# A gated cross-attention and ternary feed-forward block: the context projections of all four batches ahead of the first gate product, with every engine's order written anew

## The reference

```python
qp = ctx @ Wq.T + bq;  kp = ctx @ Wk.T + bk
scores = qp @ kp.T * 128**-0.5 * layernorm(x)
scores = where(mask, -inf, scores)
x = x + tanh(g0) * softmax(scores)
# feed-forward, weights ternary, activations scaled to 127 and rounded, row by row
gate = silu(qlinear(layernorm(x), w_gate))     # 512 -> 2048
up   = qlinear(layernorm(x), w_up)             # 512 -> 2048
x = x + tanh(g1) * qlinear(gate * up, w_down)  # 2048 -> 512
# qlinear: wq = clip(round(w / (mean|w| + eps)), -1, 1); xq = round(x / (max|x| / 127 + eps))
```

## Time and profile before

| | |
|---|---|
| time of the profiled execution | 218.4 us |
| its span | 216.6 us |
| TensorE busy | 201.9 us, 93% |
| VectorE busy | 185.9 us, 86% |
| ScalarE, POOL busy | 116.0 us, 102.0 us |
| mean granted TensorE clock | 0.976 of full speed |
| DMA | 32.84 MB, mean 152 GB/s |

### The profile page before, as it was taken

The page is one execution under the profiler, slowest core; times in us unless marked ns, Lnnn a source line. Parts: engine busy times, 40 slices in busy tenths (PEclk is TensorE's granted clock), DMA queues, the critical chain, the costliest instruction groups (busy, mean ns, idle before and its releaser), DMA issues.

```text
span 216.6 us, 2892 instructions
## 1 busy us (share of the span) xinstructions
PE 201.9 (93%) x862; PEld 91.4 (42%) x862; DVE 185.9 (86%) x376; ACT 116.0 (54%) x161; POOL 102.0 (47%) x152
## 2 busy tenths in 40 slices
PE   8866289999999999999999999999999999999983
PEld 7322133444444444444444444444444444444431
DVE  0899999899999999999999999999999859865711
ACT  2149988999889572296034572765442611532400
POOL 2657898880989696249732053175220520500000
PEclk9999758999999999999999999999999999999999
DMA  6999993089201380992031458002615251739991
GB/s 207 413 425 410 417 390 136 0 331 407 91 0 38 77 157 0 185 229 48 0 73 26 82 114 194 0 0 50 123 22 102 42 105 33 175 65 320 246 272 58
DMA packets 47360, 32.84 MB, mean 152 GB/s; under 512 B 40944, under 2 KB 41072, under 8 KB 45808
## 3 DMA queue, kind: packets, MB, share of 16 engines
q1 hardware_dynamic: 47200, 32.51, 52.6%
q10 hardware_dynamic: 144, 0.13, 0.4%
HBM read 18.48 MB, written 4.19 MB: 105 GB/s over the span
## 4 chain that ended last, share of the span: by engine, by line
PE 76%; DMA 11%; SPq 7%; DVE 2%; ACT 1%; ACTq 1%; issue 1%
PE pU L1024 25%; PE pG L1009 24%; PE pD L1043 21%; DMA stage_b<-in_L_ffn_w_up 9%; PE pA L976 4%; SPq L387 3%; DMA stage_b<-stage_b 2%; SPq L382 2%; ACTq L70 1%; PE pA L966 1%; PE pA L956 1%; SPq L374 1%; ACT hid L781 1%; DVE am L1385 1%; DVE hid L1381 1%
## 5 line engine op out<-in xcount | busy, mean ns | idle before, releaser
L781 ACT ACTIVATE hid<-pG,act_g 128x512 f32<-128x512 f32 x64 | 42.9, 686 | 50.2 <-PE pG L1009 41.3
L1009 PE MATMUL pG<-gate_w,xqT 128*128 128x512 f16 x256 | 62.6, 383 | 0.1
L1043 PE MATMUL pD<-down_w,stage_b 128*128 128x512 f16 x256 | 60.2, 379 | 1.1 <-DMA stage_b<-stage_b 1.1
L1024 PE MATMUL pU<-up_w,xqT 128*128 128x512 f16 x256 | 60.8, 379 | 0.0
L1376 DVE TENSOR_TENSOR hid<-pU,hid 128x512 f32<-128x512 f32 x64 | 42.1, 682 | 3.3 <-PE pU L1024 3.1
L1009 PEld LDWEIGHTS pG<-gate_w,xqT 128*128 128x128 f16 x256 | 25.0, 99 | 35.1 <-issue 7.4
L1043 PEld LDWEIGHTS pD<-down_w,stage_b 128*128 128x128 f16 x256 | 24.8, 98 | 32.5 <-issue 2.3
L1024 PEld LDWEIGHTS pU<-up_w,xqT 128*128 128x128 f16 x256 | 24.8, 98 | 30.7 <-issue 1.1
L976 PE MATMUL pA<-kT,qT 128*128 128x512 f32 x26 | 15.5, 679 | 4.5 <-DVE probs L1293 4.3
L1385 DVE TENSOR_REDUCE am<-hid 128x1 f32<-128x1025 f32 x16 | 19.3, 1211 | 0.3
L1381 DVE TENSOR_REDUCE hid<-hid 128x1 f32<-128x1024 f32 x16 | 19.3, 1206 | 0.0
(11 more groups left out here) (108 smaller groups left out, 245.7 us busy)
## 6 DMA issues: line engine op xcount, KB each, us to landing
stage_a<-in_L_ffn_w_gate SPq DMA_DIRECT2D x4, 1024.0 KB, 11.2
stage_b<-in_L_ffn_w_up SPq DMA_DIRECT2D x4, 1024.0 KB, 20.2
stage_a<-in_L_ffn_w_down SPq DMA_DIRECT2D x4, 1024.0 KB, 9.9
stage_b<-in_x SPq DMA_DIRECT2D x2, 1024.0 KB, 5.9
out<-x SPq DMA_DIRECT2D x8, 256.0 KB, 2.6
out<-stage_b SPq DMA_DIRECT2D x8, 256.0 KB, 3.4
ctx_s<-in_ctx SPq DMA_DIRECT2D x4, 256.0 KB, 8.6
x<-in_x SPq DMA_DIRECT2D x2, 512.0 KB, 5.6
```

The costliest lines, as they stand in the source:

```text
L781: act.activation(hid[:, t % NH, n * 512:(n + 1) * 512], pG[c % NG][:, :], ACT.Silu, scale=act_g[:, t:t + 1]).then_inc(silu_done, 1)
L1009: ins = pe.matmul(pG[c % NG][:, :], xqT[:, t // TILES % 2, t % TILES, k, :], gate_w[:, n, k, :], start=k == 0, stop=k == KD - 1)
L1024: ins = pe.matmul(pU[c % NU][:, :], xqT[:, t // TILES % 2, t % TILES, k, :], up_w[:, n, k, :], start=k == 0, stop=k == KD - 1)
L1043: ins = pe.matmul(pD[t % ND][:, :], hidT[:, t % 2, k, :], down_w[:, k // KD, k % KD, :], start=k == 0, stop=k == KI - 1)
```

## The change

The four products and copies for batches 2 and 3 leave pA. All q projections after the first go through bank pG1, all k projections through pG0, one after the other, and `gate(0, 0)` and `gate(1, 0)`, which are the first gate products to write these banks, wait for the copies of the last batch. `PA_ORDER` then holds only q0 and the scores.

```diff
-        q_banks = [pA, pG[1], pA, pA]
-        k_banks = [pG[0], pG[0], pA, pA]
+        q_banks = [pA, pG[1], pG[1], pG[1]]
+        k_banks = [pG[0], pG[0], pG[0], pG[0]]
...
-        CENTRE_BY = 'VPAAVAPAAPVAAVPA'
+        CENTRE_BY = 'VPAAPAPAAPVAAPPA'
...
-        HQ_BY = ['PA', 'AP', 'VP', 'PA', 'PV', 'VA', 'AP', 'VA', 'PA', 'VA', 'VP', 'PV', 'PP', 'AA', 'VV', 'AA']
+        HQ_BY = ['PA', 'AP', 'VP', 'PA', 'PV', 'AA', 'AP', 'VA', 'AA', 'VA', 'AP', 'PV', 'PP', 'VA', 'PV', 'AA']
...
-        SIGN_BY = ['VQQQ', 'QXQX', 'QXVQ']
+        SIGN_BY = ['VQQQ', 'QXQX', 'XXVQ']
...
             def project_q(b):
                 if b == 0:
                     pe.wait_ge(params_loaded, 16)
-                if b != 1:
-                    wait_pA(pe, "q", b)
+                    wait_pA(pe, "q", 0)
+                if b >= 2:
+                    pe.wait_ge(q_ready[b - 1], 1)
...
             def project_k(b):
...
-                if b >= 2:
-                    wait_pA(pe, "k", b)
-                elif b == 1:
-                    pe.wait_ge(k_ready[0], 1)
+                if b >= 1:
+                    pe.wait_ge(k_ready[b - 1], 1)
...
                 if c == 0:
-                    pe.wait_ge(k_ready[1], 1)
+                    pe.wait_ge(k_ready[B - 1], 1)
                 elif c == 1:
-                    pe.wait_ge(q_ready[1], 1)
+                    pe.wait_ge(q_ready[B - 1], 1)
```

More of the change, by code:

```diff
@@ L648, in _ @@
             residual1(6)
+            centre(4)
+            up_scales(1)
             std2(2)
@@ L653, in _ @@
             mask(2)
[L654 removed]
+            quantise_hidden(0, 0)
             gate_scales(2)
[L656 removed]
+            up_scales(2)
+            mask(3)
+            centre(6)
             std2(3)
[L658 to L659 removed]
+            weight_round(2, 3)
             quantise_hidden(1, 1)
@@ L857, in _ @@
             exp(11)
+            silu(6, 0)
+            silu(6, 1)
             silu(6, 2)
+            quantise_hidden(3, 1)
+            centre(8)
             silu(6, 3)
-            quantise_hidden(3, 1)
+            quantise_x(8)
             silu(7, 0)
             silu(7, 1)
-            centre(8)
-            quantise_x(8)
             silu(7, 2)
@@ L1180, in _ @@
             down(5, 2)
-            down(5, 3)
+            gate(9, 3)
+            up(8, 2)
+            up(8, 3)
+            up(9, 0)
             score(15)
@@ L1496, in _ @@
+            score(5)
+            weight_bound(0, 0)
             weight_bound(0, 1)
+            weight_bound(0, 2)
             absmax_x(2)
+            absmax_x(3)
             weight_abs(1, 3)
-            weight_bound(0, 2)
+            inverse_x(1)
+            stats1(6)
             weight_bound(0, 3)
-            absmax_x(3)
-            inverse_x(1)
             weight_scale(1)
-            inverse_std2(1)
-            stats1(6)
+            mask_and_max(5)
             score(6)
             stats1(7)
+            copy_xT(1)
@@ L1508, in _ @@
+            mask_and_max(6)
             weight_bound(1, 0)
             weight_bound(1, 1)
-            copy_xT(1)
             score(7)
+            mask_and_max(7)
             product(0, 0)
-            mask_and_max(4)
-            mask_and_max(5)
-            mask_and_max(6)
-            mask_and_max(7)
             product(1, 0)
             product(0, 1)
+            product(1, 1)
+            inverse_std2(1)
             weight_bound(1, 2)
-            product(1, 1)
             weight_bound(1, 3)
-            absmax_hidden(0, 0)
+            stats1(8)
@@ L1569, in _ @@
             score(10)
+            absmax_hidden(2, 0)
             weight_bound(2, 1)
-            inverse_hidden(2)
+            weight_round(2, 2)
+            score(11)
             weight_bound(2, 2)
             weight_bound(2, 3)
-            quantise_hidden(2, 0)
-            product(4, 2)
             product(4, 3)
-            absmax_hidden(3, 0)
-            residual2(0)
-            score(11)
-            mask_and_max(8)
-            mask_and_max(9)
+            absmax_hidden(2, 1)
@@ L1605, in _ @@
             absmax_x(8)
             absmax_x(9)
+            inverse_hidden(4)
             inverse_x(4)
+            quantise_hidden(4, 1)
+            stats2(10)
+            stats1(12)
+            inverse_std2(4)
+            score(12)
+            absmax_hidden(5, 0)
+            centre(10)
+            product(6, 3)
             product(7, 0)
-            quantise_hidden(4, 1)
+            mask_and_max(12)
             product(7, 1)
-            stats2(11)
-            product(7, 2)
-            absmax_hidden(5, 1)
@@ L1614, in _ @@
-            residual2(2)
-            inverse_hidden(5)
-            inverse_std2(4)
-            inverse_std2(5)
-            product(7, 3)
-            stats1(12)
-            centre(10)
-            absmax_x(10)
-            product(8, 0)
+            product(7, 2)
+            residual2(2)
+            stats1(13)
+            absmax_hidden(5, 1)
+            product(7, 3)
+            inverse_hidden(5)
+            absmax_hidden(6, 0)
+            stats2(11)
+            product(8, 0)
+            absmax_hidden(6, 1)
@@ L1636, in _ @@
-            inverse_hidden(6)
-            score(13)
-            inverse_hidden(7)
-            quantise_hidden(7, 0)
-            residual2(4)
-            stats1(14)
-            score(14)
-            mask_and_max(12)
-            stats1(15)
+            inverse_x(5)
+            absmax_hidden(8, 0)
+            stats1(14)
+            quantise_x(10)
+            residual2(4)
+            inverse_hidden(6)
+            stats1(15)
+            score(14)
+            product(8, 2)
+            absmax_hidden(7, 1)
@@ L1685, in _ @@
+            reciprocal_scale(6)
+            absmax_x(15)
+            absmax_hidden(11, 0)
+            inverse_x(7)
             product(11, 3)
             product(12, 0)
+            quantise_x(13)
+            inverse_std2(7)
+            absmax_hidden(11, 1)
+            product(12, 1)
+            inverse_hidden(9)
+            inverse_hidden(10)
+            product(12, 2)
+            product(12, 3)
+            inverse_hidden(11)
             quantise_hidden(9, 0)
-            absmax_hidden(10, 0)
```

603 lines of the change are left out of this document (286 added, 317 removed).

## The result

The changed kernel takes 220.71 us, the median of 4 runs (220.29 to 222.46), against 218.55 us for the kernel before beside it: ratio 1.0129 [1.0082, 1.0177], its 95% interval in brackets. The forecast was 217.2 us in 214.3 to 220.0. The profiled execution took 220.83 us for a span of 219.0 us, 2.4 us more than before, so its stages can be compared directly.

The account below looks back on a forecast made before the run. TensorE's remaining work was taken as the bound from about 42 us to the last tile, VectorE keeping up with nothing to spare. 218.4 - 3.45 + 2.6 + 0.6 - 1.0 = 217.15, forecast 217.2 us, range 214.3 to 220.0.

Parts of the forecast that it names:

- term 2: Start: the first gate products wait for the q3 copy, so the first up product comes 2.6 us later (1.4 to 3.3).
- term 3: Middle: relief for VectorE gains nothing by itself; waiting at `down(2, 0)` and small stalls cost 0.6 us (0 to 2.8).
- term 4: End: more cover for the last tile's chain and a store out of the way win 1.0 of 1.07 us.
- Term 1: Dense stretch of TensorE, from 45.28 us: four projections of 0.86 us each taken out win 3.45 us.
- what would make me wrong altogether: Middle: gaps spread over TensorE, each released by VectorE, would mean VectorE had become the bound; no size or chance given.
- The second limit: Start: VectorE's bound of up chunk 0, behind three masks and a copy, makes the first up product 2.2 to 3.1 us later.
- the sum by the rule: Middle: VectorE and GpSimd block each other, so centres given to POOL could make the total about 0.5 us worse.
- The start is not late: Rival, chance 0.27: q3 and VectorE's bound come in time, the late start vanishes; 213.9 us, or 215.2 with half of it.
- TensorE stands at `down(2, 0)`: Rival, chance 0.17: TensorE waits 2.8 us there for `residual2(0)`; 220.35 us, or 219.35 if the last tile's chain closes.

Follow-up runs that it names:

- e6: Kernel before with the four projections of batches 2 and 3 and their copies left out, not moved; 218.45 us, ratio 1.0002.
- e10: Changed kernel with one VectorE instruction, mask_and_max(4), moved behind weight_scale(1), nothing left out; 217.28 us, ratio 0.9974.
- e1: Kernel before with only the four projections moved, with their banks, waits, copies and context loads; other calls keep their places; 220.51 us, ratio 1.0102.
- e12: e10 with tile 14's second maximum and inverse ahead of tile 15's first maximum, and inverse_hidden(8) ahead of two residuals; 217.38 us, ratio 0.9979.
- e4: Changed kernel with ScalarE's rounding of tile 8's first half moved behind the silu of tile 11's first chunk; 224.69 us, ratio 1.0296.
- e17: Kernel before with store(10) to store(13) moved behind the last transposition on SP's queue; 217.2 us, ratio 0.9945.
- e2: Changed kernel with the last q copy (ScalarE) and the up chunk's half sum (VectorE) moved earlier; 221.55 us, ratio 1.0143.
- e7: e1 with 24 unused matmuls filling TensorE's wait for the first silu, to hold its clock; 220.97 us, ratio 1.013.

## Why the forecast was wrong

By the ledger the change came out 3.6 us above the forecast's sum: 1.4 us by term 2, 1.2 by term 3, 1.0 by term 4. Three steps failed: the price of the late start left out VectorE's waits for POOL, the middle was priced by one place that cost almost nothing, and the end took one store out of the way of the last transpositions and overlooked three others.

- **Term 1** was right as a row (3.45 us of TensorE's work left) and unsafe as a gain. "A microsecond taken out of that stretch is a microsecond won, if nothing else becomes late" failed in its condition in the old orders: e6 returned 3.05 of 3.45 us as idle time, 2.4 of it in waits for VectorE. In the changed kernel and in e10 TensorE has none of those four gaps. No run has the new orders without the move, so what the move is worth in them isn't shown. The earlier trace rows had said it for the kernel before, 14.93 of 15 us; I read that as keeping up with nothing to spare, and then gave TensorE the whole gain. The sentence on what would make me wrong altogether (gaps released by VectorE) describes the stretch up to 68 us in e1 and e6, and had no chance in the list.
- **Term 2** is the largest miss: +4.04 instead of +2.6 us. Its working was wrong twice, with opposite signs. I counted four gate products between `gate(1, 0)` and the up sum; the list has two, and without the collisions of VectorE and POOL the sum comes at 37.11 us and the first up product at 43.00 us (e10), 0.5 us late instead of 2.6. The second limit was off too: with the same three masks ahead of it, the first bound of the up chunks ran at 42.22 us in e10 and 41.59 before, 0.6 us later and not 2.5 to 3.4. What made the term 4.04 is 3.3 us of VectorE standing behind POOL's long roundings, which the working of this term did not contain at all.
- **That price** was in the text, but in term 3, where the sum by the rule was put at 0.5 us worse. The Trainium skill (SBUF — State Buffer, Who interferes with whom) says that VectorE in a two-port mode and GpSimd exclude each other for a whole instruction, and so do VectorE with two inputs in SBUF and a GpSimd instruction that reads SBUF. By that, what matters is the length of the other's instruction: the price is up to 2 us for each meeting with a chunk's rounding (1.97 us alone on POOL in e10), not the 0.6 us that the earlier trace rows showed for two short ones. The trace agrees in both places: 2.45 for 0.75 us, and 3.59 for 1.97.
- **Term 3**: 1.8 instead of 0.6 us. The place that I priced, `down(2, 0)`, cost 0.11 us: `residual2(0)` ran at 96.03 us. The idle time stood elsewhere, 0.35 us at 111.88, 0.85 at 148.27, 0.35 at 157.25. No run takes all of it away; e12 and e4 remove the largest and get others.
- **Term 4**: nothing won of 1.0 us. I put it down to the last tile's chain and one store; e17 shows both gaps of before to be SP's queue. The change took the store between tile 15's transpositions away, but left three ahead of tile 14's. There they cost 0.56 us of the 0.86: the half was rounded at 202.70 us and its transposition issued at 203.26.
- **Rivals.** "The start is not late" is what e10 shows of the start (0.5 us), and even so the time was 217.3 and not 213.9 us: the rival's sum had nothing for the middle, where e10 stands 1.9 us, and 1.07 us won at the end, where it stands 1.6 us instead of 1.4. The clock was higher too, as this rival has it: 1.00 from 30 to 35 us in the change, 0.56 before. Whether the four projections did that isn't shown, since e10, with the same ones, had 0.50 from 30 to 32 us; term 2 had already counted its gate products at the higher level. "TensorE stands at `down(2, 0)`" gave a time near the measured one for a reason that did not occur. That the forecast of 217.2 us and e10's 217.28 agree is an accident: e10 has -3.45, +0.47 and 2.1 us more idle time of TensorE.

What stays open: why TensorE's clock fell in e2 and not in the change, how the waits of e6 would spread if VectorE were relieved in the stretch from 45 to 68 us alone, what the lower clock in e1 costs by itself, and what the move is worth in the new orders.

## What to carry to other kernels

When two engines are both over 95% busy in a stretch, price a relief of one at nothing until the other one's rows at the very place of the removed work have been read; leaving the work out is the cheapest test of it. When orders are rewritten, set VectorE's residuals, which read two arrays in SBUF, and its passes over 16-bit weights against POOL's long instructions, side by side: here the place of one mask cost 3.4 us. At the end of a kernel read the issuing queue before the compute chain: here, moving stores that nobody waits for behind the last transposition was worth 0.5% in the kernel before.

## What the runs showed of the hardware

- A VectorE residual of 0.75 us that meets a POOL rounding of about 2 us waits it out (2.45 us), while statistics (0.66 us) and a sum of magnitudes over one array (1.20 us beside a 1.97 us rounding, e10) do not notice it. The mask, with two inputs in SBUF, started 0.2 us ahead of POOL's rounding in the change; POOL's two roundings then took 4.79 us, 4.35 in e10.
- TensorE stood idle for 2.87 us ahead of its scores in the change and for 2.44 us in e2, and was granted 1.00 of its clock after the first and 0.50 (1.2 GHz) after the second; after 2.47 us in e4 it was granted 0.50 too. Twelve gate matmuls took 4.71 us in e2, 4.55 in e1 (0.75) and 2.92 in e7 (1.00), so the lower level cost up to 1.8 us on these twelve.
- Issuing one transposition took SP's queue 1.23 to 1.89 us, 1.29 in the median, from 193 us on in e17, and a store 0.33 to 0.63, 0.45 in the median (0.33 to 0.97 in the kernel before). The merged rows of several, such as 7.22 us for four, hold waits too: in that one SP waited 1.8 us for ScalarE's rounding.
